# Pairwise products for 40 fields and an MLP: 24 of 50 batches by samples, alternating; VectorE's sums spread; eight gathers in a row for the first eleven duos

## The reference

```
e = stack([tbl_f[ids[:, f]] for f in range(40)], axis=1)       # 2048 x 40 x 64
p, q = e[:, rowidx], e[:, colidx]                              # 780 pairs r < c
z = einsum('bie,fie,bif->bi', p, param, q)                     # param: 64 x 780 x 64
h = maximum(concat([z, dense_ctx]) @ W_top1 + b_top1, 0)       # 796 -> 512
h = maximum(h @ W_top2 + b_top2, 0)                            # 512 -> 256
y = h @ W_top3                                                 # 256 -> 1
```

## Time and profile before

| | |
|---|---|
| median of 3 runs | 1384.01 us (1381.89 to 1385.51) |
| profiled execution | 1380.23 us, its span 1378.2 us |
| busy | TensorE 90%, VectorE 75%, ScalarE 51%, GpSimd 44% |
| granted TensorE clock, mean | 0.968 of full speed |

### The profile page before, as it was taken

The page is one execution under the profiler, slowest core; times in us unless marked ns, Lnnn a source line. Parts: engine busy times, 40 slices in busy tenths (PEclk is TensorE's granted clock), DMA queues, the critical chain, the costliest instruction groups (busy, mean ns, idle before and its releaser), DMA issues.

```text
span 1378.2 us, 20032 instructions
## 1 busy us (share of the span) xinstructions
PE 1242.5 (90%) x6032; PEld 435.1 (32%) x6032; DVE 1032.1 (75%) x899; ACT 697.6 (51%) x5257; POOL 604.4 (44%) x646
## 2 busy tenths in 40 slices
PE   0446799989899999999999999999999999999999
PEld 0112233233233333333333333333333333333333
DVE  0124687878887878888887878888887888888970
ACT  0013366475554366484555366485555366485441
POOL 4555555555555554555555555554454454000000
PEclk9777899999999999999999999999999999999999
DMA  3111122222222222222222222222222222111100
GB/s 124 26 34 43 49 66 57 65 57 62 60 64 59 65 58 64 57 70 60 58 65 60 63 58 65 58 71 57 56 64 65 53 59 62 41 52 47 47 10 0
DMA packets 50531, 77.55 MB, mean 56 GB/s; under 512 B 14004, under 2 KB 14260, under 8 KB 50296
## 3 DMA queue, kind: packets, MB, share of 16 engines
q1 hardware_dynamic: 29936, 55.26, 13.9%
q0 software_dynamic: 20480, 21.01, 7.9%
q10 hardware_dynamic: 8, 0.01, 0.0%
HBM read 76.22 MB, written 0.01 MB: 55 GB/s over the span
## 4 chain that ended last, share of the span: by engine, by line
PE 68%; DVE 3%; ACT 3%; issue 1%; another core or an unknown queue 0%; DMA 0%; POOL 0%; DVEq 0%
PE ring L476 28%; PE z_ps L495 14%; PE ring L482 12%; PE aux L414 5%; ACT act_prod L327 3%; DVE prod L400 2%; PE aux L446 2%; PE ring L414 2%; PE aux L421 2%; PE ring L477 1%; DVE sums L367 1%; PE aux L428 1%; PE ring L421 0%; DVE dve_prod L400 0%; PE aux L435 0%
## 5 line engine op out<-in xcount | busy, mean ns | idle before, releaser
L400 DVE TENSOR_TENSOR prod<-ring,emb 128x1024 f32<-128x1024 f32 x544 | 636.3, 1218 | 285.9 <-PE ring L477 264.0
L327 ACT ACTIVATE act_prod<-act_prod 128x64 f32<-128x64 f32 x2560 | 611.7, 242 | 144.0 <-DVE act_prod L400 110.6
L282 POOL DMA_INDIRECT stage<-tbl,idx x512 | 482.8, 943 | 450.5 <-issue 242.0
L476 PE MATMUL ring<-emb,raw 64*128 64x512 f32 x1088 | 570.9, 639 | 34.2 <-DVE prod L400 23.2
L477 PE MATMUL ring<-emb,raw 64*128 64x512 f32 x1088 | 571.9, 641 | 0.0
L327 ACT ACTIVATION_READ_ACCUMULATOR act_prod<-act_prod 128x1 f32 x2560 | 482.8, 189 | 2.3 <-issue 2.0
L476 PEld LDWEIGHTS ring<-emb,raw 64*128 64x128 f32 x1088 | 182.3, 192 | 376.9 <-issue 212.7
L495 PE MATMUL z_ps<-prod,sel 128*32 128x512 f32 x2176 | 262.4, 600 | 1.3 <-DVE prod L400 1.3
L482 PE MATMUL ring<-raw,emb 64*128 64x512 f32 x512 | 247.7, 614 | 4.1 <-DVE prod L400 3.1
L483 PE MATMUL ring<-raw,emb 64*128 64x512 f32 x512 | 247.8, 614 | 0.0
L294 ACT ACTIVATE emb<-aux 128x512 f32<-128x512 f32 x80 | 47.4, 592 | 316.4 <-PE aux L446 284.9
(11 more groups left out here) (32 smaller groups left out, 199.3 us busy)
## 6 DMA issues: line engine op xcount, KB each, us to landing
raw<-param_b SPq DMA_DIRECT2D x200, 256.0 KB
stage<-tbl,idx POOLq DMA_INDIRECT x512
kept<-tbl,idx POOLq DMA_INDIRECT x128
W<-W1g SPq DMA_DIRECT2D x1, 1792.0 KB
W<-W2t SPq DMA_DIRECT2D x1, 512.0 KB
idx<-ids_t SPq DMA_DIRECT2D x1, 240.0 KB, 3.6
z<-dense_t SPq DMA_DIRECT2D x4, 32.0 KB, 2.6
idx<-ids_t SPq DMA_DIRECT2D x1, 80.0 KB, 2.0
```

What stands on the lines that cost most here:

```text
L282: pool.indirect_dma_start(to[:, t, E * (f % 2) : E * (f % 2) + E], None, tables[f], bass.IndirectOffsetOnAxis(ap=idx[:, c, f, t : t + 1], ...
L327: op = act.activation(part, part, ACT.Copy, accum_out=sums[:, t, at : at + 1])
L400: dve.tensor_tensor(to, ring[:, n % RING, :, :], by, ALU.mult).then_inc(prod_done, 1)
L476: pe.matmul(ring[:, n % RING, 0, :], w[0:E], emb[0:E, PLACE[c, m], :], start=True, stop=True)
```

## The change

**The mix.** The kept rows are now those of the first eight duos, in two halves of four. Batches by samples are (duo m, half): for duos 4 to 11 the first half, for 12 to 19 both. There are 24 of them, and 26 by fields. After the first two batches by fields the two kinds alternate. The number of units stays 200 a chunk, and so do the seven groups that layer 1 reads. There are three groups of turned sums a chunk instead of two, and `sums` has two places that are used in turn.

**The sums.** VectorE sums nine of the 24 batches, ScalarE fifteen. VectorE's `tensor_reduce` comes after every fourth product instead of bunched behind its batch; ScalarE's order is planned with at least three units from one sum to the next (`ACT_AT`). In the last chunk the last batch by samples is summed by ScalarE; before it was VectorE.

**The other uses of `aux`.** The tiles of layer 1 come before units 38, 54, 78 and 94 (before: 24, 60, 96 and 132), those of layer 2 before units 118 and 142, layer 3 before unit 166 (before: 168, 192 and 199). Units 54 and 94 have a duo at the same place, as unit 96 had before. Duos 7 and 8 are turned 4 units later in the program than before, all from duo 9 on 8 units later (duo 23 before unit 164 of chunk 0 instead of 156).

**The gathers.** For the first eleven duos the eight gathers are issued in a row, without the wait behind the fourth.

```diff
-KEPT = 4
-ROWS = 2 * KEPT
+ROWS = 8
+ROW_DUOS = ROWS // 2
+HALVES = 2
+KEPT = HALVES * ROW_DUOS
 BATCH = 4
+SAMPLES = []
+for _m in range(ROW_DUOS, DUOS):
+    SAMPLES.append((_m, 0))
+    if _m >= 12:
+        SAMPLES.append((_m, 1))
 FIELD_UNITS = []
...
-    FIELD_UNITS += [("full", _m, _k) for _k in range(KEPT if _m >= KEPT else 0, _m)]
+    _from = ROW_DUOS * sum(1 for _x, _h in SAMPLES if _x == _m)
+    FIELD_UNITS += [("full", _m, _k) for _k in range(_from, _m)]
...
-NS = DUOS - KEPT
-DVE_SUMS = [KEPT + i for i in (1, 4, 7, 10, 13, 15)]
-ACT_SUMS = [m for m in range(KEPT, DUOS) if m not in DVE_SUMS]
+NS = len(SAMPLES)
+DVE_SUMS = [i for i in range(NS) if i % 8 in (1, 4, 6)]
+ACT_SUMS = [i for i in range(NS) if i not in DVE_SUMS]
...
 for _j in range(NF):
     BATCHES.append(("fields", _j))
-    if _j % 2 and _j // 2 < NS:
-        BATCHES.append(("samples", KEPT + _j // 2))
+    if _j and _j <= NS:
+        BATCHES.append(("samples", _j - 1))
...
+GROUPS = [("fields", 0), ("samples", 0), ("fields", 1), ("samples", 1), ("fields", 2), ("samples", 2), ("fields", 3)]
...
+SUM_PLACES = 2
 RING = 3
-PROD = 2 * BATCH
-DPROD = 3
+PROD = 7
+DPROD = 4
 APROD = 6
...
-ZS = 11
+ZS = 9
...
+HASTY = 11
...
-    AUX_AT.setdefault(NU * _c + BATCH * (AT["samples", 11] + 3), []).append(("turn", _c, 0))
+    for _g in range(SGROUPS if _c < NCH - 1 else SGROUPS - 1):
+        _at = NU * _c + BATCH * (AT["samples", PER_GROUP * (_g + 1) - 1] + 6)
+        AUX_AT.setdefault(_at, []).append(("turn", _c, _g))
 for _c in range(NCH - 1):
-    AUX_AT.setdefault(NU * (_c + 1) + BATCH, []).append(("turn", _c, 1))
-    for _m, _x in zip(DVE_SUMS, [("h1", _c, 0), ("h1", _c, 1), ("h1", _c, 2), ("h1", _c, 3), ("h2", _c, 0), ("h2", _c, 1)]):
-        AUX_AT.setdefault(NU * (_c + 1) + BATCH * (AT["samples", _m] + 1), []).append(_x)
-    AUX_AT.setdefault(NU * (_c + 2) - 1, []).append(("y", _c, 0))
+    for _b, _x in ((9, "h1"), (13, "h1"), (19, "h1"), (23, "h1"), (29, "h2"), (35, "h2"), (41, "y")):
+        _n = sum(1 for x in AUX_AT.values() for y in x if y[:2] == (_x, _c))
+        AUX_AT.setdefault(NU * (_c + 1) + BATCH * _b + 2, []).append((_x, _c, _n))
...
-            SUM_AT[NU * _c + BATCH * _b + (8 if _b + 1 < NB and BATCHES[_b + 1][0] == "samples" else 6)] = (_c, _x)
+            SUM_AT[NU * _c + BATCH * _b + 6] = (_c, _x)
+        elif _x in DVE_SUMS:
+            for _t in range(BATCH):
+                REDUCE_AT[NU * _c + BATCH * _b + 1 + BATCH * _t] = (_c, _x, _t)
...
+ACT_AT = {}
+_at = 0
+for _c in range(NCH):
+    for _i in ACT_SUMS:
+        for _t in range(BATCH):
+            _at = max(_at + 3, 4 * (NB * _c + AT["samples", _i] + 1) + 2 * _t)
+            ACT_AT.setdefault(_at // 4, []).append((_c, _i, _t))
 PLACE = {}
...
-                    if i == FLIGHT:
+                    if i == FLIGHT and n >= HASTY:
...
+                for x in ACT_AT.get(n, ()):
...
+            def reduce(c, i, t):
+                tenant = sums_tenant(c, i)
+                if t == 0 and tenant[0] >= 0:
+                    dve.wait_ge(aux_ready, AUX_NO["turn", tenant[0], tenant[1]] + 1)
+                dve.wait_ge(prod_done, NU * c + BATCH * AT["samples", i] + t + 1)
...
-                    by = kept[:, c % 2, t : t + 1, :].to_broadcast([P, 2, CH])
+                    by = kept[:, c % 2, SAMPLES[x][1], t : t + 1, :].to_broadcast([P, 2, CH])
...
-                if unreduced:
-                    reduce(*unreduced)
-                unreduced = (c, x, t) if kind == "samples" and x in DVE_SUMS else None
-                if unreduced and t == BT - 1:
-                    reduce(*unreduced)
-                    unreduced = None
+                if n in REDUCE_AT:
+                    reduce(*REDUCE_AT[n])
```

More of the change, by code:

```diff
@@ L151, in fm_mlp_kernel @@
         idx = sb("idx", [P, NCH, FIELDS, BT], I32)
-        kept = sb("kept", [P, 2, BT, KEPT * P])
+        kept = sb("kept", [P, 2, HALVES, BT, ROW_DUOS * P])
         stage = sb("stage", [P, STAGE, BT, P])
@@ L158, in fm_mlp_kernel @@
         dve_prod = sb("dve_prod", [P, DPROD, 2, CH])
-        sums = sb("sums", [P, BT, NS * 2 * ROWS])
+        sums = sb("sums", [P, BT, SUM_PLACES * P])
         z = sb("z", [P, ZS, CH])
@@ L316, in save_z @@
                 act.activation(z[:, z_place(c, "fields", g), :], z_ps[:], ACT.Copy).then_inc(z_saved, 1)
-            def reduce(c, m, t):
-                g = (m - KEPT) // PER_GROUP
-                if c:
-                    act.wait_ge(aux_ready, AUX_NO["turn", c - 1, g] + 1)
-                act.wait_ge(prod_done, NU * c + BATCH * AT["samples", m] + t + 1)
+            def reduce(c, i, t):
+                tenant = sums_tenant(c, i)
+                if tenant[0] >= 0:
+                    act.wait_ge(aux_ready, AUX_NO["turn", tenant[0], tenant[1]] + 1)
+                act.wait_ge(prod_done, NU * c + BATCH * AT["samples", i] + t + 1)
                 for j in range(2 * ROWS):
                     at = E * (j % ROWS)
-                    part = act_prod[:, sampled(c, m, t) % APROD, j // ROWS, at : at + E]
-                    at = sums_of(m).start + j
+                    part = act_prod[:, sampled(c, i, t) % APROD, j // ROWS, at : at + E]
+                    at = sums_of(c, i).start + j
                     op = act.activation(part, part, ACT.Copy, accum_out=sums[:, t, at : at + 1])
@@ L330, in _ @@
             for n in range(NCH * NB):
-                for t in reversed(range(BT)):
-                    c, b = divmod(n - 1 - t, NB)
-                    if c >= 0 and BATCHES[b][0] == "samples" and BATCHES[b][1] in ACT_SUMS:
-                        reduce(c, BATCHES[b][1], t)
+                for x in ACT_AT.get(n, ()):
+                    reduce(*x)
                 for u in range(BATCH * n, BATCH * n + BATCH):
@@ L342, in _ @@
             last = NCH - 1
+            for n in range(NCH * NB, max(ACT_AT) + 1):
+                for x in ACT_AT.get(n, ()):
+                    reduce(*x)
             save_z(last, FGROUPS - 1)
             act.wait_ge(tail_ready, 1)
-            act.activation(z[:, z_place(last, "samples", 1), :], aux[:], ACT.Copy).then_inc(tail_saved, 1)
+            act.wait_ge(stored, 16 * last)
+            act.activation(z[:, z_place(last, "samples", SGROUPS - 1), :], aux[:], ACT.Copy).then_inc(tail_saved, 1)
             for m in range(H1 // P):
@@ L354, in _ @@
             act.wait_ge(tail_ready, 1 + H1 // P + H2 // P + 1)
[L355 to L356 removed]
+            act.activation(y_out, aux[0:1, :], ACT.Copy).then_inc(tail_saved, 1)
             act.wait_ge(tail_saved, 1 + H1 // P + H2 // P + 1)
[L358 removed]
+            act.dma_start(out_v[last : last + 1, :], y_out).then_inc(stored, 16)
             act.wait_ge(stored, 16 * NCH)
@@ L362, in _, with reduce @@
         def _(dve):
-            def reduce(c, m, t):
-                if c and t == 0:
-                    dve.wait_ge(aux_ready, AUX_NO["turn", c - 1, (m - KEPT) // PER_GROUP] + 1)
-                dve.wait_ge(prod_done, NU * c + BATCH * AT["samples", m] + t + 1)
-                dve.tensor_reduce(
-                    sums[:, t, sums_of(m)], dve_prod[:, sampled(c, m, t) % DPROD, :, :].rearrange("p a (j e) -> p (a j) e", e=E), AX.X,
-                    ALU.add,
-                ).then_inc(dve_reduced, 1)
+            def reduce(c, i, t):
+                tenant = sums_tenant(c, i)
+                if t == 0 and tenant[0] >= 0:
+                    dve.wait_ge(aux_ready, AUX_NO["turn", tenant[0], tenant[1]] + 1)
+                dve.wait_ge(prod_done, NU * c + BATCH * AT["samples", i] + t + 1)
+                made = dve_prod[:, sampled(c, i, t) % DPROD, :, :].rearrange("p a (j e) -> p (a j) e", e=E)
+                dve.tensor_reduce(sums[:, t, sums_of(c, i)], made, AX.X, ALU.add).then_inc(dve_reduced, 1)
             dve.memset(sel[:], 0.0).then_inc(sel_zero, 1)
@@ L434, in turn_sums @@
                 for t in range(BT):
-                    mm = pe.transpose(aux[:, P * t : P * t + P], sums[:, t, P * g : P * g + P], ident[:])
+                    mm = pe.transpose(aux[:, P * t : P * t + P], sums[:, t, sums_place(c, g) : sums_place(c, g) + P], ident[:])
                 return mm
@@ L547 @@
                 for h in range(2):
-                    r, c = 2 * i + h, 2 * x + side
+                    m, half = SAMPLES[x]
+                    r, c = ROWS * half + 2 * i + h, 2 * m + side
                     param_b[b, side, :, i, h] = param[:, pair_index(r, c)]
-                    g, row = divmod(2 * ROWS * (x - KEPT) + ROWS * side + r, P)
+                    g, row = divmod(2 * ROWS * x + ROWS * side + 2 * i + h, P)
                     W1g[row, GROUP_NO["samples", g]] = W["W_top1"][pair_index(r, c)]
```

49 lines of the change are left out of this document (26 added, 23 removed).

## The result

| | before | after | predicted |
|---|---|---|---|
| median us, runs on one chip | 1382.95 (4 runs) | 1407.66 (4 runs) | 1344 |
| ratio, 95% interval | | 1.0178 [1.0148, 1.0209] | 0.971 |
| profiled execution, span | 1380.2, 1378.2 | 1408.68, 1406.9 | 1340.3, 1338.3 |
| duo 30's last gather | 445.25 | 420.75 | 420.2 |
| duo 30 turned | | 429.86 | 422.7 |

The change makes the kernel 1.8% slower; 3% faster was forecast. A chunk is counted here on VectorE, from the start of its first product to the start of its last one; that is one step of 1.13 us less than from chunk to chunk, so the forecast's 307 stands as 306. The first product comes 6.7 us earlier and chunk 0 is 349.2 us (before 379.1), so the start gives 36.6 us; chunks 1 to 3 lose 61.9 and the end 3.4.

The account below looks back on a forecast made before the run. Gathers were taken to bound the start up to about duo 30, then VectorE. Unit 236 at 425.4 plus 870 us of chunks gives 1295.4; with 42.9 for the end, 2.0 around the span and 3.8 to the median, 1344 us, range 1314 to 1370.

Parts of the forecast that it names:

- The gathers: First eleven duos: without the wait behind the fourth gather 25 us are saved, bounds 0 to 27.
- Which unit a duo releases: Chunk 0: gathers set the pace to about duo 30 and release 8 more units; the start gives 47.3 us with the gathers' 25.
- The end: After the last product: ScalarE's last sums make TensorE wait 3.3 us more, 42.9 us instead of 39.55.
- A chunk in the steady stage: From unit 236 on: VectorE is the slower engine, 266.7 + 36.4 + 4 = 307 us a chunk, ends 293 and 320.
- VectorE's 266.7 us: Steady chunk: 236 VectorE steps of 1.13 us, including twelve more sums.
- +4: Steady chunk: ScalarE's copies before units 54 and 94 come up to 2 us late each, 4 us a chunk, between 0 and 8.
- 8.0: VectorE's idle at 26 blocks of row sums a chunk: 18 with a sum just ahead cost nothing, 8 cost 1.0 us each.
- TensorE's 14.2 us a chunk: Steady chunk: TensorE loses eight blocks of row sums and gains one turning, 14.2 us less work.
- ScalarE and VectorE late: Rival: copies hold `aux` at more places and row sums cost VectorE 1.0 us everywhere; chunk 320, 1380 us or 1362; chance 0.13.
- TensorE the bound: Rival: TensorE stays the bound and each chunk gives its 14.2 us back, 1304 us, half way 1320; chance 0.15.
- Eight gathers bring nothing: Rival: in the start the 25 us from the removed wait are missing, 1369 us; chance 0.07.
- The clock rival: Chunks 1 to 3: TensorE waiting for VectorE is granted clock 0.93, chunk 326, 1397 us, slower than before; chance 0.06.

Follow-up runs that it names:

- numbers 6: Kernel after with the wait behind the fourth gather put back for the first eleven duos: 1.0312 of the kernel before.
- number 7: Kernel before with eight gathers in a row for the first eleven duos and nothing else of the change: 0.982 of the kernel before.
- number 4: The kernel after unchanged, run once more on one chip: 1.0189 of the kernel before, median 1408.42 us.
- number 5: number 3 unchanged, run once more on the same chip as number 4: 0.9923 of the kernel before, median 1372.22 us.
- numbers 12: number 3 with VectorE summing only 8 of 64 numbers in three of its nine batches: 0.9767 of the kernel before.
- number 13: number 3 without nine of the 26 blocks of row sums a chunk: 0.9744 of the kernel before.
- 14: number 3 with both VectorE's sums cut to 8 of 64 numbers in three batches and nine blocks of row sums left out: 0.9595, median 1325.98 us.
- number 3: Kernel after with ScalarE's sums listed by units and layer 1's second and fourth tiles moved to units 62 and 102: 0.9867 of the kernel before.
- number 8: Kernel after with VectorE's sums bunched behind their batch again: 1.056 of the kernel before.
- number 16: number 3 with eight gathers in a row for all twenty duos of chunk 0: 1.0032 of the kernel before.
- number 15: Kernel before with eight gathers in a row for all twenty duos of chunk 0: 0.9739, 1322.62 us against 1357.29.

## Why the prediction was wrong

*The gathers.* Right in size. Steps of 1.25 us, as forecast, duo 30's last gather at 420.75 for 420.2, and 17 to 22 us in numbers 6 and 7 for the 25 (which had bounds 0 and 27). Its reason was too wide: the first four gathers of all had a wait of 6.41 us behind them and the later ones 2.2, so landing does not take the same time in the first duo. After the change the first wait, behind eight, is 3.52 us.

*Which unit a duo releases.* Right that eight more units are released by a gather, wrong that the gathers set the pace up to there: duo 30 is turned 9.1 us after its last gather begins, not 2.5, and TensorE begins unit 236 at 434.3 us for 425.4.

*The end.* 43.0 for 42.9 us, in part by luck. TensorE waits 1.84 us before it turns the last sums, and the block of row sums ahead of them takes 3.51 us instead of 1.85, behind a wait of 3.39 us. The second profile of the same kernel (number 4) has 45.8.

```profile
1365.19 3.51 PE L524 MATMUL z_ps<-prod,sel 128*32 128x512 f32 x16 [3.39 <-DVE prod L433]
1370.54 0.63 PE L464 MATMUL aux<-ident,sums 128*128 128x128 f32 x4 [1.84 <-issue]
```

*A chunk in the steady stage.* This is the step that failed, in the idle terms added to VectorE's 266.7 us. At the last product the kernel is 68.5 us late (1363.9 for 1295.4), 9 of it by unit 236, 59 from there on. Two terms were too small.

The first is ScalarE's, "+4" between 0 and 8. Numbers 4 and 5 put it at 14, 10 and 9 us, 33 in all where 12 were forecast. The working had the mechanism and the place: 24.3 us of ScalarE's work, in fact 25.6 (847.87 to 873.47, with two idles of 0.45 between its passes), against 21.8 for TensorE, in fact 20.8 (from the end of the tile at 847.8 to 868.57). So the copy was to be 1.9 us later than the 1.23 allowed for, and was 3.6. A difference of two sums near 20 us moves by nearly its own size when each is off by 5%. The price was also read too low: what a late copy costs VectorE is the wait, then the tile that runs longer at the lower clock, together about 5 us each time (9.77 less 4.68).

The second and larger one is "8.0" for the 26 blocks of row sums: 18 at nothing, since a sum stands just ahead, and 8 at 1.0 us. Number 5 has the copies mended. Its VectorE is idle 52.1, 53.7 and 42.6 us in chunks 1 to 3 where 36.4 were forecast (counted from start to start of two instructions, less the step of 1.13). The idles up to four units behind a block, put down to that block, come out so over the three chunks:

| | forecast us | number 5 us |
|---|---|---|
| 54 blocks of row sums with a sum just ahead | 0 | 35.4 |
| 24 blocks of row sums without | 24 | 36.5 |
| 12 tiles of layer 1 | 69 | 58.8 |
| layers 2 and 3 | 16 | 16.6 |

So a sum ahead does not hide the block: 0.66 us is left each time, and a block without one costs 1.5 us. A ring that isn't full when the block begins explains little of it. In number 5 it held three units, the one in work counted, at 36 of the 54 blocks, with 0.62 us of idle each, and two at the other 18, with 0.73. TensorE makes a unit in 0.92 us where VectorE takes 1.13, so it gains 0.2 us a unit, and has to earn a block of 1.85 us or a turning back before the next one. That this short lead is the reason is argued: no run changed the ring, and numbers 12 to 14 show only that less work on either engine shortens the chunk. It would also be where TensorE's 14.2 us a chunk went: in numbers 3 and 5 VectorE has 13.6 us more work and TensorE 14.2 less, and chunks 1 and 2 are 8 to 15 us longer than in number 7.

*The rivals.* "ScalarE and VectorE late" named the cause. Its price of 320 a chunk was short of 333, 328 and 318, and did not follow from its own terms: 307 and 18 us for 18 more blocks are 325 before any copy is counted, which gives 1344 + 2.8 x 18 = 1394. "TensorE the bound" is refuted by number 13: 36 blocks of row sums fewer, 67 us, bring 25 at most in the kernel of number 3. "Eight gathers bring nothing" is refuted by number 7. The clock rival foresaw a chunk of 326 but not for this reason: the windows after have 0.97 to 1.00, and the clock falls eight times from 240 us on, six of them at a late copy of 3.9 to 4.9 us. With bunched sums (number 8) the windows are at 0.91 to 0.98.

The Trainium skill (TensorE: Matmul & The Clock Gate, "A second HAM failure mode: psum-queue depth-cycling") has short idles between groups of matmuls lower the clock. At 1000 us of the kernel after TensorE is idle 8% and granted 1.00, so in that stretch it does not. Number 8 has 0.95 there at nearly the same busy share, but its clock falls at waits of 2.25 us and not after short idles alone, so it doesn't show that rule either.

What stays open, besides duo 30 and ScalarE's idles in number 16: chunks 1 to 3 of number 15 are 6 us each below number 7's. The kernel before was 1.4% faster beside number 15 than beside number 7, which would be 4 us of a chunk; the rest has no explanation.

## What to carry to other kernels

An engine that is busy 72% of the time can still cost 36 us of 1408, through the place of one short copy in its list: for each copy that frees a bank, count what stands ahead of it, and give a result that is a difference of large sums an error of the sums' size. Where two engines have nearly equal loads and a short ring between them, don't price a wait at nothing because something stands ahead of it: 54 such blocks cost 35 us here. Work taken off one engine alone returned less than half. And do one part at a time: the wait taken out of the gathers was worth more alone than all parts together.

## What the runs showed of the hardware

- A wait of 4.87 us on TensorE was followed by 4 us at a granted clock of 0.57; a block of 6.21 us took 7.58. In number 8 waits of 1.10 and 2.25 us, two units apart, were followed by 3.4 us at 0.50.
- A unit alone between blocks of another kind took TensorE 1.06 us, one among others 0.86; a piece of two matmuls of a tile took 1.06 us alone and 0.89 within the tile. So a change of kind cost 0.1 to 0.2 us.
- Eight indirect gathers in a row were issued every 1.25 us, as four were. From the second duo to the eleventh the wait behind the eighth was 2.15 to 3.26 us; in the kernel before the waits behind a fourth or an eighth were 2.16 to 2.76. The first wait of all was longer: 6.41 us behind four gathers, 3.52 behind eight.
- The same kernel, the one before, took 1357 us in one group of runs and 1377 to 1383 in the others, 1357.29 and 1381.74 on one chip by its number.
